# Eight PSUM banks split anew (2 + 3 + 3 for 2 + 2 + 4) in a four-layer attention kernel whose order is a written table

## The reference, cut to what matters

```
x += attention0(layernorm(x), ctx)      # strictly causal, own weights
x += layernorm(x) @ sign(W).T
x += attention1(layernorm(x), ctx)      # causal, with biases
x += routed experts: top 2 of 16, 256 -> 128 -> 256, silu(g)*u, + 2 shared experts
x += attention2(ctx, layernorm(x), mask)  # q, k, v layer-normed, mask from input
x += bit-linear: quantised x, ternary weights, 256 -> 1024 -> 256
x += attention3(layernorm(x), ctx, ctx) # no weights, no mask
x  = 3 blocks: h = h + qlora(gelu(layernorm(qlora(h))))
```

## Time and profile before

| what | value |
|---|---|
| median of three runs | 1161.57 us |
| the profiled execution, first to last instruction | 1166.1 us |
| mean granted TensorE clock in it | 0.970 of full speed |
| TensorE busy | 1050.5 us (90%) |
| VectorE busy | 903.8 us (78%) |
| ScalarE busy | 804.5 us (69%) |
| GpSimd busy | 564.1 us (48%) |

### The profile page before, as it was taken

One profiled execution on the slowest core, in us unless ns is written; L12 is line 12 of the kernel. 1 busy time (PEld: TensorE's weight loads), 2 busy tenths in 40 slices (PEclk: granted clock), 3 DMA queues, 4 the chain that ended last, 5 costly groups with the idle time before them and its releaser, 6 DMA issues.

```text
span 1166.1 us, 26103 instructions
## 1 busy us (share of the span) xinstructions
PE 1050.5 (90%) x8259; PEld 782.0 (67%) x8298; DVE 903.8 (78%) x3323; ACT 804.5 (69%) x1484; POOL 564.1 (48%) x1161
## 2 busy tenths in 40 slices
PE   7989999999999989898888898788898989989986
PEld 6667877777887866676666765556665665656664
DVE  3879887877564688898885588999997889887643
ACT  5757666566674555566565667656989899998962
POOL 7232364655122365577830125766455454545443
PEclk9999999999999998999999999979999999999997
DMA  7985322325667643412258864232132222222000
GB/s 239 312 284 143 92 74 56 91 74 173 203 181 210 200 127 82 136 47 84 81 185 262 249 184 147 84 92 76 39 100 73 73 55 56 83 64 55 1 19 19
DMA packets 102327, 140.03 MB, mean 120 GB/s; under 512 B 12336, under 2 KB 79792, under 8 KB 102192
## 3 DMA queue, kind: packets, MB, share of 16 engines
q1 hardware_dynamic: 98688, 129.57, 38.0%
q0 software_dynamic: 3072, 8.39, 2.3%
q10 hardware_dynamic: 432, 0.39, 0.1%
HBM read 65.43 MB, written 22.54 MB: 75 GB/s over the span
## 4 chain that ended last, share of the span: by engine, by line
PE 40%; DVE 18%; ACT 15%; DMA 8%; issue 7%; SPq 5%; POOL 5%; another core or an unknown queue 1%; DVEq 0%; POOLq 0%; ACTq 0%
PE ps L1559 9%; PE ps L1688 4%; ACT probs L2010 4%; PE ps L1580 4%; PE ps L1598 4%; SPq L2890 3%; PE ps L1781 3%; PE ps L1552 3%; PE ps L1566 2%; ACT q_st L2027 2%; DVE ps L2247 2%; DMA w<-in_expert 2%; PE ps L1601 2%; DVE ps L2255 2%; PE ps L1748 1%
## 5 line engine op out<-in xcount | busy, mean ns | idle before, releaser
L2010 ACT ACTIVATE probs<-ps 128x384 f32<-128x384 f32 (+1 forms) x512 | 260.2, 545 | 91.4 <-PE ps L1601 46.4
L1580 PE MATMUL ps<-k_st,q_st 96*128 96x256 bf16 (+1 forms) x1024 | 172.4, 266 | 26.8 <-DVE neg_max L2247 10.3
L1598 PE MATMUL ps<-q_st,k_st 104*128 104x256 bf16 (+1 forms) x1024 | 178.0, 263 | 16.8 <-ACT probs L2010 12.3
L2027 ACT ACTIVATE q_st<-ps 8x1024 bf16<-8x1024 f32 x128 | 129.9, 1016 | 24.4 <-PE ps L1669 21.8
L1580 PEld LDWEIGHTS ps<-k_st,q_st 96*128 96x128 bf16 x1024 | 86.8, 100 | 79.1 <-DVE neg_max L2247 19.1
L2247 DVE CUSTOM_DVE_ANT_0 ps<-ps,diag_s 128x128 f32<-128x128 f32 (+1 forms) x384 | 123.3, 358 | 20.9 <-PE ps L1580 18.7
L1598 PEld LDWEIGHTS ps<-q_st,k_st 104*128 104x128 bf16 x1024 | 90.7, 99 | 61.7 <-issue 19.5
L1688 PE MATMUL ps<-probs,v 128*32 128x256 f32 (+1 forms) x2048 | 126.0, 365 | 2.0 <-ACT probs L2010 1.9
L2576 POOL TENSOR_SCALAR var_eps<-mv 128x2 f32<-128x2 f32 (+1 forms) x115 | 27.8, 242 | 185.2 <-DVE mv L2139 180.1
L2255 DVE CUSTOM_DVE_ANT_0 ps<-ps,mask_s 128x256 f32<-128x256 f32 x256 | 101.4, 452 | 6.2 <-PE ps L1580 5.8
L2658 POOL CAST parts<-qf 128x512 bf16<-128x512 f32 x64 | 40.5, 633 | 100.3 <-DVE qf L2166 44.7
(11 more groups left out here) (275 smaller groups left out, 2548.9 us busy)
## 6 DMA issues: line engine op xcount, KB each, us to landing
k_st<-parts SPq DMA_DIRECT2D x192, 128.0 KB
q_st<-parts SPq DMA_DIRECT2D x189, 128.0 KB, 2.8
w<-in_expert SPq DMA_DIRECT2D x62, 384.0 KB, 4.2
x_rows<-wo SPq DMA_DIRECT2D x10, 768.0 KB, 10.9
ctx_t<-in_ctx_t SPq DMA_DIRECT2D x16, 256.0 KB, 3.0
ring<-x_rows SPq DMA_DIRECT2D x31, 128.0 KB, 3.3
y_rows<-ring SPq DMA_DIRECT2D x31, 128.0 KB, 3.7
xn_t<-x_rows SPq DMA_DIRECT2D x31, 128.0 KB, 4.0
```

What stands on the lines that cost most here:

```text
L1580: last = mm(t[:, c0:c0 + n], head(q_st, r, h, KROWS, j * P, P), head(k_st, r, h, KROWS, 0, n), start=j == 0 or not by_pe, stop=not by_pe, ...
L1598: last = mm(t[:, j * S:j * S + n], head(k_st, r, h, KALL, j * P, P), head(q_st, r, h, KALL, skip, n), start=j == 0 or L == 3, stop=L == 3, ...
L2010: nc.scalar.activation(probs[:, (hg % 2) * HPG + h4, 0:width], tile_of(key)[:, 0:width], ACT.Exp, scale=SCALE).then_inc(*tile_drained(key))
L2027: nc.scalar.activation(out, tile_of(key)[KROWS:KALL, 0:S].unsqueeze(1).to_broadcast([2 * HPG, HPG, S]), ACT.Copy).then_inc(*tile_drained(key))
```

## The change

**Banks.** "m" gets three banks and "c" three; the rule by which "c" borrows is as before.

**Order table.** Every lane's due times are new, and in hundredths of a unit in place of tenths. Of TensorE's 1,950 steps 1,890 have another place. The lanes, the steps and the items' `ORDER` are the same, and so is what each step computes. What the two tables say, read out step by step:

| | old table | new table |
|---|---|---|
| SyncE, first steps | k_stack (0,0), q_stack (0,0), load (0,2) | load (0,3), mask_load 0, mask_load 1, raw_load 0, then k_stack (0,0), q_stack (0,0), load (0,2) |
| VectorE, first steps | ln batch 0, k_rest, ln batch 1, q_rest, v_take (0,1), v_take (0,0) | ln batch 3, ln batch 0, masks 0, ln batch 1, masks 1, k_rest, v_take (0,1), q_rest, raw_sum 0, v_take (0,0) |
| TensorE steps ahead of the first maxima | 8 | 8 (k, q, v and turns of batches 0 and 1) |
| TensorE step number of the last score of (1,7) | 934 | 857 |
| steps of both expert groups' tile products | group 0 among the scores of (0,6), (1,4), (0,7); group 1 among (2,2), (2,3) | group 0 among (1,6), (1,7) and in a stretch without scores behind them; group 1 in that stretch and among (2,0), (2,1) |
| TensorE steps behind the last score | 41, with 4 block_in, 5 block_out, 4 block_turn, 3 h_turn | 35, with 2 block_in, 3 block_out, 3 block_turn, 2 h_turn |
| "s" claims of 512 at most 0.3 ahead of the bank's planned release, or later | 148 | 130 |
| "m" claims of 512, the same | 127 | 67 |
| "c" claims of 894, the same; at most 1.0 ahead | 59; 261 | 136; 410 |
| "c" claims that borrow an "m" bank | 19 | 118 |

"At most 0.3 ahead" means that the step that claims a bank is due less than 0.3 after the bank's planned release; such a claim has little slack.

**Waits.** Six places get a wait on TensorE's semaphores, or one more of them, before a buffer is written again; `wait_score` and its two calls go; `normalise` has two buffers for the inverse sums in place of one.

```diff
-        clock[0] = t / 10
+        clock[0] = t / 100
...
-        banks = {"s": (0, 1), "m": (2, 3), "c": (4, 5, 6, 7)}
+        banks = {"s": (0, 1), "m": (2, 3, 4), "c": (5, 6, 7)}
...
                 def projected(L, b):
+                    n = SLOT[L, b] - 1
+                    while n >= 0 and ORDER[n][0] == 3:
+                        n -= 1
+                    if n >= 0:
+                        wait_filled(act, ("wo", *ORDER[n]))
                     drain(("op", L, b), o_t[:, :, :])
...
                 def quantised_copy(b):
+                    if b:
+                        for T in range((b - 1) * SJ, b * SJ):
+                            for c in range(2):
+                                wait_filled(act, ("hu", T, c))
...
                 def down_copy(T):
+                    if T >= SJ:
+                        wait_filled(act, ("hd", T - SJ))
...
                     wait_filled(dve, key)
+                    if SLOT[L, b]:
+                        wait_drained(dve, ("ot", *ORDER[SLOT[L, b] - 1], pair))
+                    inv = sum_inv[:, pair, :, :]
...
-            def wait_score():
-
-                n = sum(10 * clock[0] > t for t in AT[0])
-                if n:
-                    L, b = ORDER[(n - 1) // H]
-                    wait_filled(pool, ("s", L, b, *divmod((n - 1) % H, HPG)))
...
             def load_batch(L, b):
-                if L == 0 and b >= 4:
-                    wait_filled(sp, ("v", 1, b - 4))
+                read = b - 4 if L == 0 else b + 4
+                if L == 0 and b >= 4 or L == 2 and b < 4:
+                    for what in ("k", "v"):
+                        for layer in range(2):
+                            wait_filled(sp, (what, layer, read))
                 if L == 2:
-                    if b < 4:
-                        wait_filled(sp, ("v", 1, b + 4))
-                    else:
+                    if b >= 4:
+                        for what in ("k", "v"):
+                            wait_filled(sp, (what, 2, b - 4))
                         sp.wait_ge(*part_rest.at(("k", 3, b - 4)))
...
                     if GT <= i < GT + RING:
-                        wait_filled(sp, ("logit", LAST))
-                        wait_filled(sp, ("ed", LAST))
+                        for b in (B - 2, LAST):
+                            wait_filled(sp, ("logit", b))
+                            wait_filled(sp, ("ed", b))
```

More of the change, by code:

```diff
@@ L107, in step, with drain @@
         return self.sem, self.unit
+    def drain(self, key):
+        return self.sem, self.unit
     def at(self, key):
@@ L1257, in build @@
         own = sb("own", [P, HPG], BF16)
-        sum_inv = sb("sum_inv", [P, SJ, 2 * HPG])
+        sum_inv = sb("sum_inv", [P, 2, SJ, 2 * HPG])
         bn = sb("bn", [P, 3, NT, 6])
@@ L1429, in tile_drained @@
             new_drain_at[key] = clock[0] + DRAIN
-            return drained[bank_of[key]].sem, 1
+            return drained[bank_of[key]].drain(key)
         def wait_filled(eng, key):
@@ L2280, in normalise @@
                     wait_filled(dve, key)
+                    if SLOT[L, b]:
+                        wait_drained(dve, ("ot", *ORDER[SLOT[L, b] - 1], pair))
+                    inv = sum_inv[:, pair, :, :]
                     t = tile_of(key).rearrange("p (a h e) -> p a h e", a=SJ, e=DPAD)
-                    V.reciprocal(sum_inv[:, :, :], t[:, :, :, DH]).then_inc(*inverted.step((L, b, pair)))
+                    V.reciprocal(inv, t[:, :, :, DH]).then_inc(*inverted.step((L, b, pair)))
                     dve.wait_ge(*inverted.at((L, b, pair)))
                     out = o_tok[:, r, :, pair * 2 * HPG * DH:(pair + 1) * 2 * HPG * DH].rearrange("p a (h d) -> p a h d", d=DH)
-                    V.tensor_tensor(out, t[:, :, :, 0:DH], sum_inv[:, :, :].unsqueeze(3).to_broadcast([P, SJ, 2 * HPG, DH]), ALU.mult).then_inc(
+                    V.tensor_tensor(out, t[:, :, :, 0:DH], inv.unsqueeze(3).to_broadcast([P, SJ, 2 * HPG, DH]), ALU.mult).then_inc(
                         *tile_drained(key))
@@ L2801, in scatter @@
                             pool.wait_ge(*filling.at(11))
-                    wait_score()
                     G.indirect_dma_start(x_rows[b // NB], bass.IndirectOffsetOnAxis(ap=dest[:, b * SJ + a, k:k + 1], axis=0),
```

## The result

The changed kernel takes **1189.07 us** (median of four runs, 1188.51 to 1194.16) where the kernel before takes 1160.38 us in the same comparison: a ratio of **1.0254, 95% interval 1.0213 to 1.0295**. It is slower by 2.5%. 1136 us was predicted, with a range of 1118 to 1166.

A forecast was written before the change was run, and what follows sets the result against it. TensorE, busy 90% of 1166.1 us, was taken as the bound, its 115.6 us idle time as changeable. Terms +6 - 9 - 1.5 + 9 - 9 - 16 - 5 = -25.5 gave 1140.6 us profiled, 1136 us median, range 1118 to 1166.

The forecast's parts named there:

- the start: First loads and stacks: batch 3's norm first delays the first maxima by 9 us, part comes back; +6, bounds +3 to +10.
- the middle: 400 to 800 us: a third of TensorE's 48.2 us idle time goes as expert tiles are reordered; -16, bounds +5 to -30.
- The banks: Waits for PSUM banks, priced per close claim: "m" -9, "s" -1.5, "c" +9 (0 to +35); about even.
- rival A: Three "c" banks too few: long holders (`values`, `hidden`) make transposes wait; over +46 us, 1174 to 1197 us; chance 0.10.
- if the middle keeps its 48: Sign of being wrong: TensorE's idle time from 400 to 800 us stays at 48, not the expected 30 to 35 us.
- rival B: No change: idle time only moves, the start's loss stays, VectorE near its bound in the middle; 1155 to 1164 us; chance 0.16.
- The tail: Behind the last exponential: 9.2 us of TensorE's work moves into holes elsewhere; -9, bounds -4 and -11.
- At nothing: Added waits, removal of `wait_score` and second buffer of sums, on several engines: no effect on the time.
- The clock: TensorE's half-rate stretches, 400 to 800 us: less idle time means fewer falls; -5, bounds +10 and -12.
- Rival C: TensorE's clock falls more often as tighter "c" claims idle it in short pieces; 1160 us; chance 0.06.
- Rival D: Banks of the maxima: "c" borrows one 118 times, so "m" gains -4.5 for -9; 1141 us, inside the forecast's 0.68.

The follow-up runs named there:

- new_fills: The changed kernel with only its twelve fills (expert rows' memory set to zero) moved later, behind the crowded start: 1176.52 us, 1.0133 to the kernel before.
- new_start: The changed kernel with late fills, masks, raw loads and batch 3's norm behind the first stacks, layer 1's remaining constants behind the second item's: 1166.42 us, 1.0121.
- new_late: new_fills with the second expert group's 31 tiles moved later, from 498-628 to 511-628.5 in the table: 1204.81 us, 1.0389 to the kernel before.
- new_free: new_fills with the second expert group reading the first group's rows and weights, so not waiting for its own routing: 1177.13 us, 1.0195 to the kernel before.
- old_early: The kernel before with its twelve fills earlier, five ahead of the second item's k stack, seven behind its q stack: 1158.53 us, 1.0018.

## Why the prediction was wrong

The forecast for the traces was -25.5 us; they show +21.2: idle time +19.7 up to 100 us, -0.3 to 400, -0.8 to 800 and +3.9 behind, and 1.3 us less of work. Two terms failed most: the start, +6, whose loads were followed only to the first item, and the middle, -16, of which nothing came.

**The start: the mechanism was right, the term stopped too early.** BATCH_NORM_STATS2 came at 12.66 us (forecast 13.2), the first stack at 19.99 (21), the first maxima at 33.0 (30 to 31). But the term was +6, "part comes back", because the masks were done by then. It did not come back. SyncE's queue was followed only up to the first item's stacks; read to the second item's it shows five fills, 3.9 MB, ahead of a stack. Measured: the idle time of the first 100 us rose by 19.7 us, of which `new_fills` takes back 11.8 (22.1 us are left) and 12.6 us of the time. All the moves of the start together, `new_start`, take back 1.3%, some 15 us. By the trace the term was to be near +20, by the runs near +15, both beyond its upper bound of +10.

**The banks: forecast even, measured as a loss, in the old order.** "m" was to give 9 us; its waits for row maxima fell by 4.6 us in the changed kernel, and the idle time ahead of the maxima by 5.9 and 15.0 us in the two pairs of the old order. "s" gave 5.9 us for 1.5 in the changed kernel. "c" was priced at +9, by the waits of the other two kinds; in the old order it is 20.0 and 21.8 us. There the division costs 1.1 and 1.2%, 11 to 14 us, where "about even" was forecast for the new one; how many close claims the old order has was not counted, so the price of one claim stays unknown. The mechanism is that of **rival A**: a transpose waits for a long-held tile. The rival named `values` and `hidden` as the holders, and `hidden` is the largest of them; its 46 us, 0.47 us for each of 98 claims, were twice what was measured. In the changed kernel `hidden_mult` (L2512 and L2515) ends some 9 us of idle time ahead of kind "c", where it was 2 before.

**The middle: failed.** "A third of 48 us" was a hope taken from the share of another stretch. The prediction itself named the sign of its failure, "if the middle keeps its 48", and it kept 47.4. Of the 16 us nothing came: the order moved the waits (the stretch without scores has one of 9.66 us). This is **rival B** in this part. Which property of the new order keeps the idle time as long as it was stays open; `new_late` and `new_free` only rule out the wait for the routing.

**The tail: shorter as forecast, but nothing saved by it.** From the last exponential's end, 1144.9 us, to the last instruction's, 1185.2 us, are 40.3 us and were 50.6: -10 for a forecast of -9. The term also needs the moved work to fall into holes of TensorE, and it did not. The stretches from 800 us to the last exponential and from there to the end, of the kernel before and then of the changed one:

```profile
800.00:1113.30 313.30, 286.19 (x2266) 194.09 (x2281) 262.14 (x723) 284.00 (x450) 162.49 (x326) 0.99 0.22 63
1113.30:1166.10 52.80, 40.37 (x190) 29.90 (x188) 24.11 (x64) 19.15 (x40) 23.22 (x44) 0.89 0.04 16
```

```profile
800.00:1144.90 344.90, 312.56 (x2448) 215.83 (x2447) 296.79 (x789) 305.75 (x484) 173.57 (x349) 0.99 0.20 57
1144.90:1187.30 42.40, 31.39 (x152) 22.71 (x152) 19.96 (x52) 15.91 (x33) 17.85 (x34) 0.90 0.05 19
```

TensorE works 9.0 us less in the tail, but its idle time there falls only from 12.4 to 11.0 us, and ahead of the tail it rises from 27.1 to 32.3.

**At nothing: the waits nearly right, `wait_score` wrong.** The added waits cost 0.4%, some 4 us, in the old order. `wait_score` was worth 8 us: its 4.0 us of the earlier trace rows were only a part of the scatters' waits, and two groups of fetches waited too, 4.2 and 5.1 us in the kernel before.

**The clock: the gain of 5 did not come.** The trace has 0.962 for 0.970; the four timed executions have 0.957 to 0.970, those of the kernel before 0.970 to 0.983. In the trace the loss is in the start (0.80 for 0.95 over the first 100 us, 0.52 from 60 to 70 us, behind the 10.04 us of standing still); from 100 us on it is 0.98, and was 0.97. What the lower clock costs there was not separated from the waits. **Rival C** did not come: after the start no stretch of 100 us is below 0.91, and before had 0.90. The page named there (the Trainium skill, TensorE: Matmul & The Clock Gate, "A second HAM failure mode: psum-queue depth-cycling") expects low clock from cycling through the banks; `old_banks`, whose one change is the division, with fewer banks for the cycling products of kind "c", has 0.971 to 0.980 in its executions against 0.970 to 0.980 in those of the kernel before beside it, so nothing here shows it.

**Rival D**, the lending, was not tested by itself; the waits for row maxima fell by 4.6 us, as it has it (4.5).

## What to carry to other kernels

Follow every queue that a new order touches up to the second use of the critical transfer, not only the first: bulk loads that nobody waits for are free only until something urgent stands behind them. Price a bank by how long its holders keep it, not by how close the claims lie: here a bank taken from tiles that wait for a busy engine cost 20.0 and 21.8 us and gave 5.9 and 15.0 to the maxima. Work moved out of the tail is saved only if it falls into idle time elsewhere. Change one thing at a time where you can; here a gain of 0.3%, the waits without `wait_score`, lay hidden under the losses, and the old order with it and with late fills beats both kernels.

## What the runs showed of the hardware

Issuing itself became slow in some stretches with full DMA engines. In the changed kernel the six issues of a k stack took SyncE 4.10 us at 19.99 us and 6.77 us at 46.90 us behind five fills; in `old_early` they took 6.29 us at 30.11 us behind five fills, in `new_fills` 5.95 us at 41.20 us behind none (305 GB/s from 40 to 50 us). The fills took 0.94 us each at 42.15 us (five in 4.70 us; 336 GB/s from 40 to 50 us) and 1.80 us each at 53.71 us (seven in 12.62 us, two of them small; 404 to 412 GB/s), and 0.54 to 0.89 us each where `new_fills` has them, from 117 to 163 us. So SyncE's own program was held up too, and every load and stack behind it. Full engines alone do not do it: in the kernel before, two stacks at 25.54 and 29.54 us took 3.96 and 4.04 us with the engines full (324 GB/s), and one at 69.21 us took 4.98 at 415 GB/s. What limits the issue was not tried apart.
